# Rotation of the keys on one engine, key parts stored once, and the last query set projected between the first score steps: an attention and LoRA block on one core

## The reference

```python
def _apply_rope(x, cos, sin):
    xr = x[..., 0::2]; xi = x[..., 1::2]
    out_r = xr * c - xi * s
    out_i = xr * s + xi * c
q = _apply_rope((x @ wq).reshape(bsz, 256, 32, 16), cos, sin)
k = _apply_rope((x @ wk).reshape(bsz, 256, 8, 16), cos, sin)
v = (x @ wv).reshape(bsz, 256, 8, 16)           # k and v are repeated 4 times over the heads
scores = einsum('bqhd,bkhd->bhqk', q, k) / 4 + causal_mask
out = einsum('bhqk,bkhd->bqhd', softmax(scores), v) @ wo
x = x + layernorm(attention(layernorm(x)))
x = x + layernorm(ffn(layernorm(x)))
```

## Time and profile before

| what | us |
|---|---|
| three runs, median | 234.1 |
| lowest and highest of the three | 232.86 and 234.14 |
| the profiled execution, its own time | 233.25 |
| span of the profiled execution | 231.5 |
| step 0 begins (first score matmul) | 52.68 |
| step 5 begins | 65.05 |
| step 20 begins | 102.28 |

### The profile page before, as it was taken

The page is one execution under the profiler, slowest core; times in us unless marked ns, Lnnn a source line. Parts: engine busy times, 40 slices in busy tenths (PEclk is TensorE's granted clock), DMA queues, the critical chain, the costliest instruction groups (busy, mean ns, idle before and its releaser), DMA issues.

```text
span 231.5 us, 3767 instructions
## 1 busy us (share of the span) xinstructions
PE 202.0 (87%) x1304; PEld 122.8 (53%) x1304; DVE 173.6 (75%) x364; ACT 116.8 (50%) x207; POOL 115.4 (50%) x102
## 2 busy tenths in 40 slices
PE   0599999998878979999999989899889989997860
PEld 0484834444444444444444424145778878996840
DVE  1882616867998896859696885685898898898885
ACT  3340531243124877878766785773578335343231
POOL 8200333553357795797743446462756275323352
PEclk9999999999999999999999999999999999999996
DMA  5998049977985102795762203354230000110113
GB/s 166 381 363 338 3 136 204 256 201 167 193 206 144 38 1 72 185 193 103 171 118 65 49 11 51 96 96 96 47 98 0 3 19 26 47 48 0 45 45 136
DMA packets 22465, 26.73 MB, mean 115 GB/s; under 512 B 3760, under 2 KB 17328, under 8 KB 21680
## 3 DMA queue, kind: packets, MB, share of 16 engines
q1 hardware_dynamic: 22304, 26.38, 44.8%
q10 hardware_dynamic: 144, 0.13, 0.2%
HBM read 17.19 MB, written 6.95 MB: 104 GB/s over the span
## 4 chain that ended last, share of the span: by engine, by line
PE 44%; DVE 29%; issue 9%; ACT 8%; DMA 5%; SPq 3%; POOL 1%; DVEq 0%; ACTq 0%; POOLq 0%
PE ps L1046 10%; DVE stats L777 5%; PE ps L1141 5%; PE ps L1156 5%; PE ps L1056 4%; PE ps L1204 4%; DVE nmax L977 3%; PE ps L1115 3%; PE ps L1032 3%; DMA region_b<-q_scr 3%; DVE nmax L974 2%; PE ps L1095 2%; ACT region_a L724 2%; PE ps L1110 2%; DMA x_sb<-x 2%
## 5 line engine op out<-in xcount | busy, mean ns | idle before, releaser
L544 POOL TENSOR_SCALAR_AFFINE_SELECT region_a<-region_a 128x1024 f32<-128x1024 f32 x32 | 36.9, 1153 | 27.4 <-ACT region_a L724 27.1
L977 DVE TENSOR_REDUCE nmax<-ps 128x4 f32<-128x1024 f32 x32 | 39.1, 1222 | 10.3 <-PE ps L1115 10.0
L724 ACT ACTIVATE region_a<-ps 128x1024 f32<-128x1024 f32 x32 | 32.7, 1022 | 0.2 <-PE ps L1141 0.2
L1046 PE MATMUL ps<-region_a,region_c 128*128 128x512 f32 x64 | 29.0, 598 | 0.0
L1141 PE MATMUL ps<-region_b,kst 98*128 98x512 bf16 x96 | 26.9, 381 | 1.6 <-ACT region_a L724 1.1
L721 ACT ACTIVATE region_a<-ps 128x512 f32<-128x512 f32 x32 | 19.2, 599 | 16.9 <-PE ps L1141 16.2
L974 DVE TENSOR_REDUCE nmax<-ps 128x4 f32<-128x512 f32 x32 | 21.8, 682 | 5.1 <-PE ps L1099 4.7
L1156 PE MATMUL ps<-region_a,v_aug 128*32 128x512 f32 x192 | 25.3, 603 | 0.0
L588 ACT ACTIVATE std<-mv,eps_sb 128x1 f32<-128x1 f32 x32 | 9.4, 294 | 29.7 <-DVE mv L778 29.7
L536 POOL TENSOR_TENSOR x_sb<-x_sb,region_b 128x512 f32<-128x512 f32 x8 | 10.2, 1276 | 24.8 <-ACT region_b L651 24.8
L463 POOL TENSOR_TENSOR region_a<-region_a 128x512 f32<-128x512 f32 x4 | 6.5, 1627 | 27.6 <-DVE region_a L825 27.6
(11 more groups left out here) (107 smaller groups left out, 413.9 us busy)
## 6 DMA issues: line engine op xcount, KB each, us to landing
q_scr<-region_c SPq DMA_DIRECT2D x24, 128.0 KB, 2.6
region_b<-q_scr SPq DMA_DIRECT2D x8, 384.0 KB, 4.9
x_sb<-x SPq DMA_DIRECT2D x8, 256.0 KB, 5.8
region_b<-q_scr SPq DMA_DIRECT2D x8, 256.0 KB, 5.6
attn_t<-o_sb SPq DMA_DIRECT2D x32, 64.0 KB, 2.3
rden_bc<-r_scr SPq DMA_DIRECT2D x8, 256.0 KB, 3.4
out<-region_b SPq DMA_DIRECT2D x7, 256.0 KB, 2.0
kst<-k_scr SPq DMA_DIRECT2D x8, 192.0 KB, 3.1
```

What stands on the lines that cost most here:

```text
L544: pool.affine_select(out=blocks, in_=blocks, compare_op=ALU.is_ge, fill=0.0, base=0, pattern=[[0, 2], [0, REP], [1, P]], channel_multiplie ...
L724: nc.scalar.activation(probs[:, u % PRING, 1:3, :], ps[:, 4:6, :], ACT.Exp, scale=float(HEAD_DIM) ** -0.5).then_inc(exp_done, 1)
L977: nc.vector.tensor_reduce(nmax[:, gi % 2, 1, heads], ps[:, 1:3, :].rearrange("p a (r k) -> p r a k", r=REP), AX.XY, ALU.max, negate=True). ...
L1046: last = nc.tensor.matmul(ps[:, SET_BANKS[i][ri], :], wq_sb[:, c, col:col + P], xn_t[:, c, half * HALF:(half + 1) * HALF], start=(c == 0), ...
```

## The change

It leaves what is computed as it is, and alters who does it, in which order, and how the keys are stored.

1. Keys are rotated and split by DVE alone, both halves; POOL leaves set K out. Sets 0 and 2 stay shared between DVE (real) and POOL (imaginary). Set 3 goes to POOL wholly after its products: difference, sum and the four subtractions.
2. `proj_psum` counts halves instead of sets, so DVE begins the two products of a real half while PE still projects the imaginary one (`rope_real`, `rope_products`). The real products of set 3 stand before the last subtraction of set 2.
3. `k_scr` holds each key part once, `[BATCH, PARTS, HEAD_DIM, KV_HEADS, SEQ]`. `write_k` makes 64 x 2 x 256 transfers; SP issues the six of batches 0 and 1, and ACT the six of batches 2 and 3, between its casts of set K. `load_k` is three DMAs that read a part once for each of its three, two or one copies.
4. `load_q(1)` is cut into two halves of the heads, three DMAs each; `scores(6)` waits for the second half.
5. `MATMULS_4` is (2, 2, 2, 1, 1): all eight matmuls of set 4 run in steps 0 to 4, none ahead. `scores(0)` waits for the products of sets 0 to 2 alone, `scores_more(0)` for the real products of set 3, and `scores_t(0)` for all of them.

```diff
-ROPE_3 = {0: 1, 1: 2}
-
-MATMULS_4 = (1, 1, 1, 1, 1)
+MATMULS_4 = (2, 2, 2, 1, 1)
...
-        k_scr = nc.dram_tensor("k_scr", [2, SROWS, KV_HEADS, HALF], BF16, kind="Internal").ap()
+        k_scr = nc.dram_tensor("k_scr", [BATCH, PARTS, HEAD_DIM, KV_HEADS, SEQ], BF16, kind="Internal").ap()
...
+        def write_k(engine, part, half):
+
+            i = set_of["K"]
+            dst = k_scr[2 * half:2 * half + 2, part].rearrange("b (i f) h n -> i (f h) b n", i=2)
+            for ri in range(2):
...
+                rows = parts[64 * half:64 * half + 64, i % 2, ri, part, :].rearrange("p (b n) -> p b n", b=2)
+                engine.dma_start(dst[ri], rows).then_inc(k_written[half], 16)
...
             def load_k(gi):
                 b, g = divmod(gi, 2)
-                sp.wait_ge(k_written[b // 2], WRITES_K)
+                sp.wait_ge(k_written[b // 2], WRITES)
                 wait_ring(gi)
-                sp.dma_start(kst[0:SROWS, gi % RING, :, :],
-                             k_scr[b // 2, :, g * GROUP_KV:(g + 1) * GROUP_KV, (b % 2) * SEQ:(b % 2 + 1) * SEQ])\
-                    .then_inc(qk_loaded[gi % RING], 16)
+                for part, (first, count) in enumerate(RUNS):
+                    rows = k_scr[b, part, :, g * GROUP_KV:(g + 1) * GROUP_KV, :].rearrange("r h n -> r (h n)")
+                    sp.dma_start(kst[first * HEAD_DIM:(first + count) * HEAD_DIM, gi % RING, :, :],
+                                 rows.unsqueeze(0).broadcast_to([count, HEAD_DIM, GROUP_KV * SEQ]))\
+                        .then_inc(qk_loaded[gi % RING], 16)
...
             for part in range(PARTS):
-                for half in range(2):
-                    write_k(part, half)
+                write_k(sp, part, 0)
             load_k(0)
             load_k(1)
             write_q(2)
-            load_q(1)
+            load_q(1, slice(0, GROUP_HEADS // 2))
+            load_q(1, slice(GROUP_HEADS // 2, GROUP_HEADS), second_half)
...
-            for i in range(len(SETS) - 1):
+            for i in (0, 2, 3):
                 a = i % 2
 
+                halves = (1,) if i < 3 else (0, 1)
...
+                if i == 3:
+                    pool.wait_ge(part_l[i - 2][0], 1)
+                    pool.tensor_tensor(rot[:, a, 0, :], rope_t[:, a, 0, :], rope_t[:, a, 1, :], ALU.subtract)\
+                        .then_inc(rotated[i][0], 1)
...
             for i in range(1, 4):
                 split_high(i)
+                if SETS[i] == "K":
+                    write_k(act, 0, 1)
                 split_middle(i)
+                if SETS[i] == "K":
+                    write_k(act, 1, 1)
+                    write_k(act, 2, 1)
...
+            for i in range(3):
+                rope_real(i)
+                rope_products(i, 1).then_inc(rope_mul, 1)
+                for ri in (0, 1) if SETS[i] == "K" else (0,):
                     dve.wait_ge(rope_mul, i + 1)
...
+                    rope_sum(i, ri)
+                for ri in (0, 1) if SETS[i] == "K" else (0,):
+                    rope_left(i, ri)
+                if i == 2:
+                    rope_real(3)
+                for ri in (0, 1) if SETS[i] == "K" else (0,):
+                    rope_low(i, ri)
+            rope_products(3, 1).then_inc(rope_mul, 1)
...
-            project(4, 0, 2 * KC - sum(MATMULS_4))
-
...
+                if n == GROUP_KV + GROUP_KV // 2:
+                    pe.wait_ge(second_half, 16 * len(RUNS))
...
-                    pe.wait_ge(rope_mul, 4)
+                    pe.wait_ge(rope_mul, 3)
...
+                    pe.wait_ge(real_mul, 4)
```

More of the change, by code:

```diff
@@ L329, in write_q @@
                         else:
-                            sp.wait_ge(part_l[ri], i + 1)
+                            sp.wait_ge(part_l[i][ri], 1)
                         sp.dma_start(dst[part, ri], parts[:, i % 2, ri, part, :].rearrange("p (b n) -> p b n", b=2))\
                             .then_inc(scr_written[i], 16)
-            def write_k(part, half):
-                i = set_of["K"]
-                first, count = RUNS[part]
-                dst = k_scr[half].rearrange("(s i f) h n -> i (f h) s n", s=TERMS, i=2)
-                for ri in range(2):
-                    if part == 0:
-                        sp.wait_ge(part_h, 2 * i + 1 + ri)
-                    elif part == 1:
-                        sp.wait_ge(part_m, 2 * i + 1 + ri)
-                    else:
-                        sp.wait_ge(part_l[ri], i + 1)
-                    rows = parts[half * 64:half * 64 + 64, i % 2, ri, part:part + 1, :]
-                    sp.dma_start(dst[ri, :, first:first + count, :], rows.broadcast_to([64, count, HALF]))\
-                        .then_inc(k_written[half], 16)
             def wait_ring(gi):
@@ L598, in split_high @@
                 a = i % 2
-                for ri, ready in enumerate((rot_r, rot_i)):
+                for ri in range(2):
                     if i == 4:
@@ L845, in _, with rope_real, rope_products @@
-            for i in range(3):
-                for step in range(3):
-                    rope(i, step)
-            rope(3, 0)
+            def rope_real(i):
+                if i >= 2:
+                    dve.wait_ge(rotated[i - 2][0], 1)
+                    dve.wait_ge(rotated[i - 2][1], 1)
+                rope_products(i, 0).then_inc(real_mul, 1)
+            def rope_products(i, ri):
+                a, tab = i % 2, 2 if SETS[i] == "K" else 0
+                cos, sin = (tab_sb[:, tab + j, :].unsqueeze(1).broadcast_to([P, 2, SEQ]) for j in range(2))
+                val = ps[:, SET_BANKS[i][ri], :].rearrange("p (b n) -> p b n", b=2)
+                dve.wait_ge(proj_psum, 2 * i + ri + 1)
+                for j, table in ((0, cos), (2, sin)) if ri == 0 else ((1, sin), (3, cos)):
+                    last = nc.vector.tensor_tensor(rope_t[:, a, j, :].rearrange("p (b n) -> p b n", b=2), val, table,
+                                                   ALU.mult)
+                return last
@@ new lines, in rope_sum, with rope_left @@
+            def rope_sum(i, ri):
+                a = i % 2
+                if i >= 2:
+                    dve.wait_ge(part_l[i - 2][ri], 1)
+                nc.vector.tensor_tensor(rot[:, a, ri, :], rope_t[:, a, 2 * ri, :], rope_t[:, a, 2 * ri + 1, :],
+                                        ALU.add if ri else ALU.subtract).then_inc(rotated[i][ri], 1)
+            def rope_left(i, ri):
+                a = i % 2
+                dve.wait_ge(rotated[i][ri], 1)
+                dve.wait_ge(part_h, 2 * i + 1 + ri)
+                nc.vector.tensor_tensor(resid[:, a, ri, :], rot[:, a, ri, :], parts[:, a, ri, 0, :], ALU.subtract)\
+                    .then_inc(left[i][ri], 1)
@@ L1035, in project @@
                                                         start=(c == 0), stop=(c == KC - 1))
+                        last.then_inc(proj_psum, 1)
                 else:
@@ L1048, in project @@
                                                 start=(c == 0), stop=(c == KC - 1))
-                if first + count == 2 * KC:
-                    last.then_inc(proj_psum, 1)
+                        if c == KC - 1:
+                            last.then_inc(proj_psum, 1)
             def project_v(t):
```

113 lines of the change are left out of this document (52 added, 61 removed).

## The result

| what | us |
|---|---|
| changed kernel, median | 240.51 |
| before, median of the runs beside it | 233.48 |
| ratio, with its 95% interval | 1.0255 [1.0211, 1.0299] |
| profiled execution of the changed kernel: own time, span | 240.41, 238.4 |

I had predicted 231.9 with a range to 234.3. By the medians the kernel is 7.0 slower, and I was wrong by 8.6.

The account below looks back on a forecast made before the run. PE, busy for 87% of the span, was taken to bound the kernel, DVE keeping it waiting. A gain of 1.55 up to step 5 less 0.15 at step 20 gives 1.4, from 233.25 to 231.9; range 230.4 to 234.3.

Parts of the forecast that it names:

- Matmuls and reductions: Projections to step 5: three matmuls of set 4 move into steps 0 to 2, so step 5 begins 1.55 earlier.
- Set 3's three instructions, 2.1, leave steps 0 to 2 and nothing takes their place: DVE in steps 0 to 2: reductions of about 1.9 per step against PE's 3.0, so PE is the later one.
- The rotation of the keys: Keys' chain before step 0: DVE's last subtraction done at 42.6, SP's last key write issued at 43.1 to 43.7.
- A 64 KB write lands in 2.1: Key writes before step 0: the last one lands 2.1 after its issue, at 45.5.
- late keys: Rival at step 0: key stack lands at 52.2 to 52.7, step 5 comes 1.1 late, total 234.5; chance 0.1.
- With 3.1 for the last to land: Key loads before step 0: last lands in 3.1, stack stands at 49.2 to 50.0, taken as 49.5, no wait.
- So 0 to 0.35 are given back: Step 20: two more key load issues ahead of `load_q(5)` on SP cost 0 to 0.35, taken as 0.15.
- My rival at this step: Step 20: two more SP issues at 1.97 each end 3.9 later, 1.0 of it hidden, total 234.6; chance 0.05.
- There are 2 to spare: nothing: SP's queue behind the keys: `write_q(3)` ends at about 65.5, `stack_max(0)` is wanted at 67.7, so no cost.
- DVE's three instructions taken over from POOL: Keys' rotation: DVE alone does what POOL shared, three instructions, 2.1, at a place where DVE stood idle before.

Follow-up runs that it names:

- the first experiment: The changed kernel, but key loads read with sixteen rows outermost and the copies inside, query loads in the same row order: 237.61, ratio 1.0185.
- the fastest kernel: The changed kernel with keys stored three times and loaded as before, and ACT's six key writes issued after its casts of set 2: 231.37, ratio 0.9922.
- the second experiment: The changed kernel with six key loads of 32 KB per group, one per copy and without repeat, in place of three: 239.39, ratio 1.0273.

## Why the prediction was wrong, point by point

**Matmuls and reductions: the way was right, the gain too small.** With the keys stored as before and on time (231.37) step 5 begins at 62.89; I had 63.5, from 65.05. The gain is 2.16, and 2.5 counted from the start of the block of sets 2 and 3 (36.23 in this trace, 35.90 before). I took 1.55 and called 2.0 the most. "Set 3's three instructions, 2.1, leave steps 0 to 2 and nothing takes their place" holds: none of steps 0 to 4 waits for DVE. The term that was too dear is the matmul inside a step, which I took at the 0.87 of the block: steps 0 to 2, with two matmuls, take 2.88 each (step 1 from 52.95 to 55.83), where I had 3.0, and step 4, with one, takes 2.16, so a matmul adds 0.72.

**The rotation of the keys: right.** I had the h parts cast by 39.3, the last subtraction done at 42.6 and the last write issued at 43.1 to 43.7. In the changed kernel's trace they are 39.60 (38.38 plus 1.22), 42.39 (41.10 plus 1.29) and 42.95.

**"A 64 KB write lands in 2.1": wrong, 4.46 on the path.** The row was of the last four writes in a queue of twelve, issued one by one up to 48.28, long after the query loads. The new ones go out on two queues from 39.02 on, close behind six query loads of 1.5 MB together. What made the writes early put them into the crowd. With half of the query loads moved away the same writes land in 2.4, and in the kernel before, stored once and written late, in 2.1. My rival, late keys, had the times: it put the last landing at 47.8 (47.41 in the trace), the third load at 49.1 (49.06) and the stack at 52.2 to 52.7 (about 52.94). That was partly luck. Its 4.1 was the row of writes three times as large, not of small ones in traffic, and its total, 234.5, was still 6.0 short, since it knew nothing of the loads. I gave it 0.1 on the ground that half the bytes were gone. With keys stored thrice, taking ACT's six writes out of the crowd is worth 1.6 (232.95 to 231.37; 1.1 by the ratios), and moving half of the query loads out of it brings the key loads forward by 1.7.

**"With 3.1 for the last to land": the step that failed.** I took the landing of one 192 KB block load for a load with the copies outermost. The whole of part 3 was costed at two issues more per group. Its real price is 7.5 in the changed kernel and 10.1 in the kernel before (6.7 and 9.2 by the ratios), and without it the time is 232.95. It isn't mainly the 0.8 by which the last load is slower at step 0. Three engines or two carry the h and m loads of every group, and the query loads issued behind them land late too: the last one of step 20 takes 7.7 to 8.3 in all four traces with such key loads (8.28, 8.24, 8.11, 7.73), 5.85 and 5.93 in the first two experiments, where the key loads have another form or another cut, and 6.20 before. That these loads queue behind the key loads on the same few engines is how I read it; no view shows the engines one by one.

**"So 0 to 0.35 are given back" at step 20: the issues were right, the landing wasn't.** The last query load goes out at 98.55, 2.52 later than in the earlier trace rows in a program that is 2.44 late; the two issues more cost 0.1, as the 0.15 said. But the load takes 8.28 instead of 6.20. These 2.1 and the 0.1 are 2.2 of the 2.4 by which the wait grows, from 0.41 to 2.79. My rival at this step blamed the issues.

**"There are 2 to spare: nothing" on SP's queue: wrong in its times.** I had `write_q(3)` end at 65.5; it ends at 69.49 (65.78 plus 3.71). `write_q(2)` starts late, behind six key loads that take 3.94, and six more of these stand ahead of `write_q(3)`. In the changed kernel the slow steps hide this: no step waits for the maxima. In the first experiment, with the loads mended, it is worth 3.6, as `write_q(3)` on ACT shows; a part of that is this experiment's own, whose nine query loads ahead of `write_q(3)` take 0.58 to issue instead of 0.42. With one key load per group there are 2.4 to spare, as I had said.

**A term that wasn't there: the clock.** I priced a wait at its length. Step 0 begins 3.0 late and then runs at the lower level: from 53.0 to step 1 it takes 4.55 and without the fall 2.9 (the fastest kernel), so 1.7 more. The sum comes out: 62.89, which the plan reaches without these waits, plus 3.0 and 1.7 is 67.6, and step 5 is at 67.49. At step 20 it is 2.6 of waiting (7.24 late against that kernel, after 4.60 at step 5) and 1.2 for the clock (8.40 at step 21). Together 8.4 of the 9.5 by which the spans differ; the last 1.1 is spread over later steps and I haven't traced it.

## What to carry to other kernels

Before a load or store is given another shape, look at the outermost count on both of its sides: 3 or 2 there meant three or two of sixteen DMA engines here, and transfers behind it paid as well. In the windows of these traces it shows as a DMA share of 0.14 to 0.19 while someone waits. A landing time belongs to its place: if a write is issued sooner, take it from rows with the same traffic beside it, not from the row of before. And price a new wait of PE with what may follow it, since the clock can fall.

## What the runs showed that I hadn't expected

- A load with one dimension more costs more to issue too. The key loads of the changed kernel take 0.66 in the median, the single one of before 0.5; with sixteen outermost they take 0.58, and so do the query loads of that experiment, instead of 0.42, though they are only split and repeat nothing. Loads without such a dimension, in the second experiment, take 0.42. So it isn't the repeat that costs it.

```profile
L370 SPq DMA_DIRECT2D kst<-k_scr x24: 407/659/859, 47.4 to 118.8; - x24
```

- The clock doesn't follow from the length of a wait. It fell after waits of 1.87 (keys stored thrice), 2.79 and 3.00, and stayed at full after 2.15 (read row by row) and after 2.86, in the kernel before with the queries of group 2 moved:

```profile
67.00:68.00 1.00, 1.00 (x15) 0.88 (x14) 0.57 (x1) 0.00 (x0) 0.00 (x0) 1.00 1.29 247
```

In one and the same execution, that of the changed kernel with these queries moved, it fell to 0.50 after the wait of 2.45 at step 4 and stayed at 1.00 after the one of 2.46 at step 20:

```profile
67.00:68.00 1.00, 1.00 (x3) 0.46 (x3) 0.89 (x1) 0.00 (x0) 0.00 (x0) 0.50 0.81 90
```

What decides between them stays open. It may be what spreads such kernels: three of the changed kernel's runs lie between 237.4 and 240.6. No run shows that it is.

- DVE's three instructions taken over from POOL had no price that a run shows. A pair on DVE takes 1.29, 0.65 each, and its subtraction beside POOL's sum had taken 0.99.
